# A graph network's softmax pass: one-hot rows made on ScalarE by Square and Relu, and 5 and 4 columns in turn looked up on TensorE in three groups

## The chip, the cores and the metric

One core of a Trainium2 chip. The metric is the device time of one execution in microseconds (us), shown as the median of three runs.

## What is computed

Four graph layers run one after the other over 6,250 nodes and 200,000 edges that are sorted by destination, each followed by a residual sum and a layer norm. The change is in the fourth, an attention layer with a softmax over the edges of each destination:

```python
z = x @ Wn
e = edge_attr @ We
s_src = (z @ att_src)[src]
s_dst = (z @ att_dst)[dst]
s_edge = e @ att_edge
score = jax.nn.leaky_relu(s_src + s_dst + s_edge, negative_slope=0.2)
max_per = jnp.maximum(jax.ops.segment_max(score, dst, num_segments=n), NEG)
score_exp = jnp.exp(score - max_per[dst])
denom = jax.ops.segment_sum(score_exp, dst, num_segments=n)
alpha = score_exp / (denom[dst] + 1e-08)
msg = (z[src] + e) * alpha[:, None]
out = jax.ops.segment_sum(msg, dst, num_segments=n)
return out + x
```

## The kernel before

`softmax_pass` walks over the edges in 98 blocks. The 128 partitions each own a stretch of the sorted edges, and a block is the next B = 16 edges ("columns") of every partition, 2,048 edges in all. The program's loop has IT = 49 turns of two blocks, h = 0 and h = 1. The text calls them the even block and the odd block. They have buffers of their own (names that end in 0 and 1), except the products `picked`, the messages `p_msg` and the PSUM banks `p_slots`.

Every edge needs the 65 numbers of its source node (`soft_table`: 64 features and a score). They come on two ways:

- **Gathered.** For B - K columns GpSimd issues one indirect DMA per column (L1744), with indices that ScalarE copies in `stage_index` (L1750). K is `KS[h]`, before 4 and 4, so 12 columns are gathered per block. GpSimd may start on block n + 2 only when block n's rows are used (`MADE`).
- **Looked up.** For the other K columns the table is held in SBUF in seven classes of 128 rows, each row holding 7 nodes, in two parts whose sum is exact (`parts`). `one_hots` makes for each class q a 0/1 matrix `one_lo[h][:, q, :]` by comparing the spread keys with that class's row numbers (`lanes`): seven `is_equal` passes on VectorE (L1810), each over K * 128 keys in 16-bit floats. TensorE multiplies it with the table: 7 classes x 2 parts = 14 matmuls a column (L1787), into one PSUM bank a column. VectorE then multiplies the bank with the 0/1 mask of the node within its row (`one_hi`, made by L1813) in `pick` (L1838), and adds up over the 7 in `gather` (L1841).

The four looked-up columns are in two groups of two: `multiply(h, 0)` goes to the banks `p_slots[0]`, `multiply(h, 1)` to `p_slots[1]`, and `pick(0)` and `pick(1)` empty them. Between the two groups TensorE turns the edge attributes of the block (L1801, two transposes).

The order of VectorE's work for block n is written out by hand. It goes: `pick(0)`; the seven one-hot passes for block n + 1 (L1810); the mask for n + 1 (L1813); `gather(0)`; `pen` and the carried top (L1860, L1861); the attributes' part of the score, which waits for TensorE's transposes (`turned`; L1864, L1866, L1868); `pick(1)`, `gather(1)`; seven small steps for the score, the running maximum and the exponents (L1878 to L1891). There it waits for ScalarE's Exp (L1769, L1770). Then come the messages (L1895 to L1900) and the segmented running sum, a scan over 81 x 16 numbers (L1905).

ScalarE does, for block n: wait for the gathers, copy the indices of block n + 2 (L1750), wait for the exponents (`SCORED`), two Exps, spread the factors for the scan (L1772), wait for the scan's end, copy the running rows out (L1776, L1777), and copy slots, keep and at_dst of block n + 2 (`stage`, L1753 to L1755). SyncE loads keys and attributes and stores the rows.

The semaphore `stepped` counts VectorE's steps, `per` of them a block, and everybody's waits for VectorE are counts of it: `FIRST_MADE` is `pick(0)`, `SECOND_MADE` is `pick(1)`, `SCORED` the exponents, `MADE` the messages of the features. `looked` counts TensorE's finished groups.

## Time and profile before

| | us |
|---|---|
| median of 3 runs | 13501.89 |
| the runs | 13510.13, 13501.60, 13501.89 |
| the profiled execution: span, first to last instruction | 13509.6 |
| TensorE (PE) busy | 9536.4 (71%) |
| VectorE (DVE) busy | 11066.4 (82%) |
| ScalarE (ACT) busy | 4374.5 (32%) |
| GpSimd (POOL) busy | 9266.9 (69%) |

The profiled execution's time as such is not listed apart; its span is 0.5 us under the slowest of the three runs and 7.7 us over the median, 0.06%. The shares are averages over all four layers. The softmax pass is the last large stage: its gathers are issued between 11856 us and 13382 us of the span, about 1530 us or 11% of it. In the rows PE is TensorE's matmuls, PEld its weight loads, and a line such as L1787 is a line of the kernel before.

### The profile page before, as it was taken

What the parts mean: (1) busy time and instruction counts of PE and PEld (TensorE: products, weight loads), DVE (VectorE), ACT (ScalarE), POOL (GpSimd) and SP (SyncE); (2) the same over time, 40 slices, a digit from 0 to 9 for tenths busy, and PEclk for the clock granted to TensorE, in tenths of its full rate; (3) what the DMA queues carried; (4) which work ended last, traced back from release to release, by engine and by line L of the source; (5) the groups of instructions that cost most, each with busy time, mean ns of one, the idle gap of its engine ahead of it and who ended that gap; (6) DMA issues with size and microseconds to landing.
All of it is one profiled execution on the core that took longest, in us unless ns stands there. A gap on an engine that the chain in (4) does not pass through costs nothing. (4 is left out here: it accounts for less than half of the span.)

```text
span 13509.6 us, 209667 instructions
## 1 busy us (share of the span) xinstructions
PE 9536.4 (71%) x57073; PEld 8046.3 (60%) x57073; DVE 11066.4 (82%) x24500; ACT 4374.5 (32%) x14847; POOL 9266.9 (69%) x9348
## 2 busy tenths in 40 slices
PE   5666667777757766777774546886886888678886
PEld 4555556666645555555552116886886777567775
DVE  8888878888768888888888997886886888589997
ACT  3444434444423333333333331111111111123332
POOL 6777757777667777777774005777776777677776
PEclk8888879999878888888886667998997999699997
DMA  3333324444323333333335761221221222133332
GB/s 89 89 89 85 88 71 125 124 119 124 113 65 100 99 101 101 101 100 97 99 101 195 272 246 41 48 47 39 47 48 38 50 49 49 30 78 87 85 87 68
DMA packets 637171, 1243.59 MB, mean 92 GB/s; under 512 B 206033, under 2 KB 390390, under 8 KB 586530
## 3 DMA queue, kind: packets, MB, share of 16 engines
q1 hardware_dynamic: 322624, 912.21, 19.9%
q0 software_dynamic: 300160, 269.02, 11.8%
q10 hardware_dynamic: 14337, 61.82, 1.2%
q8 instruction: 16, 0.26, 0.0%
q14 instruction: 34, 0.28, 0.0%
HBM read 475.84 MB, written 768.08 MB: 92 GB/s over the span
## 5 line engine op out<-in xcount | busy, mean ns | idle before, releaser
L1030 PE MATMUL p_slots<-part,one_lo 128*128 128x208 f32 (+1 forms) x18032 | 2666.9, 312 | 616.3 <-DVE one_lo L1048 615.9
L990 POOL DMA_INDIRECT rows<-gcn_table,index x2450 | 2442.6, 997 | 883.0 <-issue 727.7
L1030 PEld LDWEIGHTS p_slots<-part,one_lo 128*128 128x128 f32 x18032 | 2584.2, 205 | 699.2 <-DVE one_lo L1048 682.7
L1351 PE MATMUL a_p_slots<-att_part,a_one_lo 128*128 128x456 f32 x8232 | 2007.5, 408 | 585.2 <-DVE y L1414 502.8
L1351 PEld LDWEIGHTS a_p_slots<-att_part,a_one_lo 128*128 128x128 f32 x8232 | 1741.4, 214 | 953.6 <-DVE y L1414 680.7
L1282 POOL DMA_INDIRECT sent<-a_out_rows,a_place x1568 | 1585.5, 1011 | 494.0 <-issue 476.2
L622 PE MATMUL p_slots<-x_part,key_lo 128*128 128x448 f32 x6916 | 1649.2, 393 | 109.7 <-DVE scratch L751 73.3
L556 POOL DMA_INDIRECT msg<-x_rows,index x1372 | 1312.0, 956 | 507.4 <-issue 448.4
L556 POOL DMA_INDIRECT msg<-h_rows,index x1274 | 1234.4, 969 | 490.9 <-issue 383.8
L622 PEld LDWEIGHTS p_slots<-x_part,key_lo 128*128 128x128 f32 x6916 | 1378.1, 206 | 226.3 <-DVE scratch L751 90.3
L788 DVE SCALAR_TENSOR_TENSOR run<-run,keep,msg 128x129 f32<-128x129 f32 (+1 forms) x3136 | 1112.8, 355 | 388.7 <-ACT msg L591 284.2
L1744 POOL DMA_INDIRECT e_rows<-soft_table,e_index x1176 | 1167.4, 993 | 375.6 <-issue 330.8
L1787 PE MATMUL e_p_slots<-soft_part,e_one_lo 128*128 128x456 f32 x5488 | 1243.9, 387 | 125.2 <-DVE e_one_lo L1810 125.2
L1787 PEld LDWEIGHTS e_p_slots<-soft_part,e_one_lo 128*128 128x128 f32 x5488 | 1073.9, 198 | 260.3 <-DVE e_one_lo L1810 146.4
L1273 POOL DMA_INDIRECT a_rows<-att_table,a_index x980 | 998.9, 1019 | 305.7 <-issue 298.4
L1048 DVE TENSOR_SCALAR one_lo<-keys,lanes 128x1152 fp32r<-128x1152 f16 (+2 forms) x1188 | 826.4, 756 | 10.6 <-DMA keys<-key_rows 10.6
L996 ACT COPY index<-src_i 128x8 int32 (+4 forms) x300 | 59.2, 198 | 2286.4 <-DMA rows<-gcn_table,index 2176.6
L591 ACT ACTIVATE msg<-msg,weight 128x64 f32<-128x64 f32 x3136 | 769.1, 340 | 0.5 <-DVE msg L769 0.5
L584 ACT ACTIVATE earlier<-p_same 128x1280 bf16<-128x1280 f32 x392 | 485.2, 1238 | 787.8 <-PE p_same L637 787.8
L1078 DVE TENSOR_TENSOR picked<-p_slots,one_hi 128x832 f32<-128x832 f32 (+1 forms) x588 | 704.1, 1198 | 37.3 <-PE p_slots L1030 27.2
L1081 DVE TENSOR_REDUCE rows<-picked 128x64 f32<-128x832 f32 (+1 forms) x588 | 702.3, 1194 | 10.1
L1367 PE MATMUL a_p_label<-w_labels,a_label 128*128 128x512 f32 x392 | 340.8, 1021 | 467.4 <-DMA a_label_row<-in_label_rows 467.4
(478 smaller groups left out, 17203.7 us busy)
## 6 DMA issues: line engine op xcount, KB each, us to landing
running_dst<-a_run SPq DMA_DIRECT2D x98, 1600.0 KB
running_src<-s_run SPq DMA_DIRECT2D x98, 1600.0 KB
running<-run SPq DMA_DIRECT2D x98, 1032.0 KB
running<-run SPq DMA_DIRECT2D x98, 1024.0 KB
running<-y SPq DMA_DIRECT2D x98, 656.0 KB
s_rows<-sent ACTq DMA_DIRECT2D x98, 584.0 KB, 7.0
begun_x<-zeros SPq DMA_DIRECT2D x98, 512.0 KB
a_xdst<-begun_x SPq DMA_DIRECT2D x98, 512.0 KB
```

Source lines behind the costliest of these rows:

```text
L556: pool.indirect_dma_start(out=msg[h][:, K + k, 0:C], out_offset=None, in_=table, in_offset=offsets(index[h][:, k:k + 1])).then_inc(gathere ...
L591: nc.scalar.activation(msg[h][:, k, C:2 * C], msg[h][:, k, 0:C], ACT.Copy, scale=weight[h][:, k:k + 1]).then_inc(weighed, 1)
L622: ins = nc.tensor.matmul(p_slots[:, bank, 0:C * WIDE_CLASS], key_lo[h][:, c, e:e + P], flat(part[:, c, :, :]), start=c == 0 and part_no == ...
L788: step(nc.vector.scalar_tensor_tensor(run[h][:, k, :], before, keep[h][:, k:k + 1], msg[h][:, k, :], ALU.mult, ALU.add))
L990: pool.indirect_dma_start(out=rows[h][:, KS[h] + k, :], out_offset=None, in_=table, in_offset=offsets(index[h][:, k:k + 1])).then_inc(gath ...
L1030: ins = nc.tensor.matmul(to, one_lo[h][:, q, e:e + P], flat(part[:, q, :, :]), start=q == 0 and part_no == 0, stop=q == CLASSES - 1 and pa ...
L1048: step(nc.vector.tensor_scalar(one_lo[h][:, q, :], keys[h][:], sig["lanes"][:, q:q + 1], None, ALU.is_equal))
L1273: pool.indirect_dma_start(out=rows[h][:, K + k, :], out_offset=None, in_=table, in_offset=offsets(index[h][:, k:k + 1])).then_inc(gathered ...
L1282: pool.indirect_dma_start(out=sent, out_offset=offsets(place[h][:, k:k + 1]), in_=out_rows[h][:, k, :], in_offset=None).then_inc(scattered ...
L1351: ins = nc.tensor.matmul(to[:, k, 0:WIDE_COLUMNS], one_lo[h][:, q, e:e + P], part[:, q, :], start=q == 0 and part_no == 0, stop=q == WIDE_ ...
L1744: pool.indirect_dma_start(out=rows[h][:, KS[h] + k, :], out_offset=None, in_=table, in_offset=offsets(index[h][:, k:k + 1])).then_inc(gath ...
L1787: ins = nc.tensor.matmul(p_slots[g][:, k, 0:WIDE_COLUMNS], one_lo[h][:, q, e:e + P], part[:, q, :], start=q == 0 and part_no == 0, stop=q ...
```

## The change

In the softmax pass alone:

- `KS` becomes (5, 4): the even block looks up five columns and gathers 11, the odd block looks up four and gathers 12. TensorE has 70 and 56 matmuls a block where it had 56.
- The columns are in three groups: 2, 2, 1 in the even block and 2, 1, 1 in the odd one. The groups go in turn to two pairs of PSUM banks, `p_slots[(h + g) % 2]`, so that group 2 waits for `pick(0)` of its own block. TensorE's transposes stand behind group 1 and not behind group 0.
- VectorE has no one-hot passes in the loop any more. It has a third `pick` and a third `gather`.
- ScalarE makes the 0/1 rows in `light`: seven passes Square(2 * key + bias), with bias = -2 * lane, a pointer operand of one number a partition; and then one pass Relu(1 - x), in place over all seven classes (3,584 or 4,480 numbers a partition). The Relu waits for the last Square by a semaphore. In the turn of block n ScalarE first waits for TensorE's end of block n - 1 (`looked`), then does `light` for block n + 1, and only then what it did before.
- TensorE waits for `lit`, ScalarE's count of finished lights, and SyncE's loads of keys do too.
- One small pass at the start of the program makes `lane_bias`.

The diff:

```diff
-    KS = (4, 4)
+    KS = (5, 4)
     GATHERED = [B - K for K in KS]
-    FIRST = 2
-    GROUPS = [[slice(0, FIRST), slice(FIRST, K)] for K in KS]
-    MOST = [FIRST, max(KS) - FIRST]
-    FIRST_MADE, ONE_HOTS = 1, 1 + WIDE_CLASSES
-    SECOND_MADE = ONE_HOTS + 8
-    SCORED = SECOND_MADE + 8
+    GROUPS = [(slice(0, 2), slice(2, 4), slice(4, 5)), (slice(0, 2), slice(2, 3), slice(3, 4))]
+    G = 3
+    FIRST_MADE = 1
+    SECOND_MADE = FIRST_MADE + 8
+    THIRD_MADE = SECOND_MADE + 2
+    SCORED = THIRD_MADE + 8
...
-        picked = [sb(f"e_picked{g}", [P, MOST[g], Z, WIDE_CLASS]) for g in range(2)]
+        picked = pair("e_picked", [P, 2, Z, WIDE_CLASS])
...
-        p_slots = [ctx.enter_context(nc.psum_tensor(f"e_p_slots{g}", [P, MOST[g], 512], F32)) for g in range(2)]
+        p_slots = [ctx.enter_context(nc.psum_tensor(f"e_p_slots{g}", [P, 2, 512], F32)) for g in range(2)]
...
+        squared, lit = sig["squared"], sig["lit"]
...
-                sp.wait_ge(stepped, INIT + per * (n - 1) + ONE_HOTS)
+                sp.wait_ge(lit.sem, lit.base + n + 1)
                 load_keys(h, n + 2)
...
+            def light(h, n, loads):
+                act.wait_ge(spread_keys[h], 16 * loads)
+                for q in range(WIDE_CLASSES):
+                    ins = nc.scalar.activation(one_lo[h][:, q, :], keys[h][:], ACT.Square, bias=sig["lane_bias"][:, q:q + 1], scale=2.0)
+                ins.then_inc(squared.sem, 1)
+                act.wait_ge(squared.sem, squared.base + n + 1)
+                nc.scalar.activation(flat(one_lo[h][:]), flat(one_lo[h][:]), ACT.Relu, bias=sig["ones"][:, 0:1], scale=-1.0).then_inc(lit.sem, 1)
...
                 stage(h, h * B)
+            light(0, 0, 1)
             with act.Fori(0, IT) as i:
...
                     n = 2 * i + h
+                    act.wait_ge(looked, G * (n + 1))
+                    light(1 - h, n + 1, i + 1 + h)
...
                     stage_index(h, (n + 2) * B)
...
             def multiply(h, g):
-                for k in range(KS[h] - FIRST if g else FIRST):
-                    e = (g * FIRST + k) * P
+                cut, to = GROUPS[h][g], p_slots[(h + g) % 2]
+                for k in range(cut.stop - cut.start):
+                    e = (cut.start + k) * P
                     for q in range(WIDE_CLASSES):
                         for part_no, part in enumerate(parts):
-                            ins = nc.tensor.matmul(p_slots[g][:, k, 0:WIDE_COLUMNS], one_lo[h][:, q, e:e + P], part[:, q, :],
+                            ins = nc.tensor.matmul(to[:, k, 0:WIDE_COLUMNS], one_lo[h][:, q, e:e + P], part[:, q, :],
                                                    start=q == 0 and part_no == 0, stop=q == WIDE_CLASSES - 1 and part_no == len(parts) - 1)
...
+            pe.sem_inc(looked, G)
             with pe.Fori(0, IT) as i:
...
-                    pe.wait_ge(stepped, INIT + per * (n - 1) + ONE_HOTS)
+                    pe.wait_ge(lit.sem, lit.base + n + 1)
+                    pe.wait_ge(stepped, INIT + per * (n - 1) + SECOND_MADE)
                     multiply(h, 0)
+                    pe.wait_ge(stepped, INIT + per * (n - 1) + THIRD_MADE)
+                    multiply(h, 1)
...
                     pe.wait_ge(loaded[h], 16 * (B // PACK) * (i + 1))
...
-                    multiply(h, 1)
+                    pe.wait_ge(stepped, INIT + per * n + FIRST_MADE)
+                    multiply(h, 2)
...
-            def one_hots(h, step):
-                for q in range(WIDE_CLASSES):
-                    step(nc.vector.tensor_scalar(one_lo[h][:, q, :], keys[h][:], sig["lanes"][:, q:q + 1], None, ALU.is_equal))
             def one_slots(h, step):
...
             nc.vector.memset(run[1][:], 0.0).then_inc(stepped, per + FIRST_MADE)
-            dve.wait_ge(spread_keys[0], 16)
-            one_hots(0, lambda ins: ins.then_inc(stepped, 1))
             dve.wait_ge(staged[0], 1)
-            one_slots(0, lambda ins: ins.then_inc(stepped, per - ONE_HOTS))
+            one_slots(0, lambda ins: ins.then_inc(stepped, per - FIRST_MADE))
             with dve.Fori(0, IT) as i:
...
                     n, done = 2 * i + h, [0]
...
                     def pick(g):
-                        many = KS[h] - FIRST if g else FIRST
-                        slots = p_slots[g][:, 0:many, 0:Z * WIDE_CLASS].rearrange("p k (c s) -> p k c s", s=WIDE_CLASS)
+                        many = GROUPS[h][g].stop - GROUPS[h][g].start
+                        slots = p_slots[(h + g) % 2][:, 0:many, 0:Z * WIDE_CLASS].rearrange("p k (c s) -> p k c s", s=WIDE_CLASS)
                         mask = one_hi[h][:, GROUPS[h][g], :].unsqueeze(2).broadcast_to([P, many, Z, WIDE_CLASS])
-                        step(nc.vector.tensor_tensor(picked[g][:, 0:many, :, :], slots, mask, ALU.mult))
+                        dve.wait_ge(looked, G * (n + 1) + g + 1)
+                        step(nc.vector.tensor_tensor(picked[g % 2][:, 0:many, :, :], slots, mask, ALU.mult))
                     def gather(g):
-                        step(nc.vector.tensor_reduce(rows[h][:, GROUPS[h][g], 0:Z], picked[g][:, 0:KS[h] - FIRST if g else FIRST, :, :], AX.X, ALU.add))
+                        step(nc.vector.tensor_reduce(rows[h][:, GROUPS[h][g], 0:Z], picked[g % 2][:, 0:GROUPS[h][g].stop - GROUPS[h][g].start, :, :], AX.X, ALU.add))
...
-                    dve.wait_ge(looked, 2 * n + 1)
...
                     assert done[0] == FIRST_MADE
-                    dve.wait_ge(spread_keys[1 - h], 16 * (i + 1 + h))
-                    one_hots(1 - h, step)
-                    assert done[0] == ONE_HOTS
...
                     one_slots(1 - h, step)
...
-                    dve.wait_ge(looked, 2 * n + 2)
...
+                    pick(2)
+                    assert done[0] == THIRD_MADE
+                    after()
+                    gather(2)
...
+        squared.base += 2 * IT + 1
+        lit.base += 2 * IT + 1
...
         sig = {n: Signal(ctx.enter_context(nc.semaphore(n))) for n in
-               ("copied", "turned", "turned_sb", "product", "saved", "fetched", "pe_step", "act_step", "dve_step", "pool_step", "moved", "rounds")}
+               ("copied", "turned", "turned_sb", "product", "saved", "fetched", "pe_step", "act_step", "dve_step", "pool_step", "moved", "rounds", "squared", "lit")}
...
         sig["iota"], sig["lanes"] = sb("iota", [P, P]), sb("lanes", [P, WIDE_CLASSES])
+        sig["lane_bias"] = sb("lane_bias", [P, WIDE_CLASSES])
...
+                    step(V.tensor_scalar(sig["lane_bias"][:], sig["lanes"][:], -2.0, None, ALU.mult))
```

What the change does to the order on three engines, in the loop of the softmax pass, even block (buffer numbers are kept: e_keys1 are the odd block's keys).

ScalarE before, from the head of the loop's turn to the copy of the running rows (y):

```order
L1750 ACT_TABLE_LOAD
L1750 COPY e_index0<-src_i 128x12
L1768 ISA
L1769 ACTIVATE e_p_msg<-e_exps0 128x16
L1770 ACTIVATE e_factor0<-e_exps0 128x32
L1771 ISA
L1772 ACTIVATE e_carried<-e_factor0 128x81x15
L1774 ISA
L1775 REGISTER_ALU
L1776 ACTIVATE y<-e_run0 128x16x81
```

ScalarE in the changed kernel, from the same place:

```order
L1763 ACT_TABLE_LOAD
L1763 ACTIVATE e_one_lo1<-e_keys1,lane_bias 128x512 x7
L1765 REGISTER_ALU
L1766 ACTIVATE e_one_lo1<-e_one_lo1,ones 128x3584
L1780 REGISTER_ALU
L1752 ISA
L1752 COPY e_index0<-src_i 128x11
L1783 ISA
L1784 ACTIVATE e_p_msg<-e_exps0 128x16
L1785 ACTIVATE e_factor0<-e_exps0 128x32
L1786 ISA
L1787 ACTIVATE e_carried<-e_factor0 128x81x15
```

In front of the index copy and the Exp of the even block now stand the Squares and the Relu for the odd block. At the odd block's turn the same stands with 128x640 and 128x4480 numbers for the even block.

TensorE before, even block, around the transposes (L1801; part0 and part1 are the table's two parts):

```order
L1787 MATMUL e_p_slots0<-soft_part0,e_one_lo0 128x456
L1787 MATMUL e_p_slots0<-soft_part1,e_one_lo0 128x456
L1798 REGISTER_ALU
L1799 ISA
L1801 MATMUL e_p_attr<-ident,e_attr_t0 128x128 x2
L1787 MATMUL e_p_slots1<-soft_part0,e_one_lo0 128x456
L1787 MATMUL e_p_slots1<-soft_part1,e_one_lo0 128x456
```

TensorE in the changed kernel, even block, around the transposes (L1822):

```order
L1803 MATMUL e_p_slots1<-soft_part0,e_one_lo0 128x456
L1803 MATMUL e_p_slots1<-soft_part1,e_one_lo0 128x456
L1819 REGISTER_ALU
L1820 ISA
L1822 MATMUL e_p_attr<-ident,e_attr_t0 128x128 x2
L1825 ISA
L1803 MATMUL e_p_slots0<-soft_part0,e_one_lo0 128x456
```

The transposes stood behind group 0 (the 28 matmuls into e_p_slots0); they now stand behind groups 0 and 1, and the third group goes to e_p_slots0 again, behind one more wait (L1825).

VectorE before, even block, from the end of the attributes' part to the first score step:

```order
L1868 TENSOR_TENSOR e_edge_score0<-e_edge_score0,e_at_dst0 128x16
L1870 REGISTER_ALU
L1838 TENSOR_TENSOR e_picked1<-e_p_slots1,e_one_hi0 128x910
L1832 REGISTER_ALU
L1841 TENSOR_REDUCE e_rows0<-e_picked1 128x2x65
L1876 REGISTER_ALU
L1832 REGISTER_ALU
L1878 TENSOR_TENSOR e_score0<-e_rows0,e_edge_score0 128x16
```

VectorE in the changed kernel, the same place:

```order
L1881 TENSOR_TENSOR e_edge_score0<-e_edge_score0,e_at_dst0 128x16
L1855 REGISTER_ALU
L1856 TENSOR_TENSOR e_picked1<-e_p_slots1,e_one_hi0 128x910
L1848 REGISTER_ALU
L1859 TENSOR_REDUCE e_rows0<-e_picked1 128x2x65
L1855 REGISTER_ALU
L1856 TENSOR_TENSOR e_picked0<-e_p_slots0,e_one_hi0 128x455
L1848 REGISTER_ALU
L1859 TENSOR_REDUCE e_rows0<-e_picked0 128x65
L1892 REGISTER_ALU
L1848 REGISTER_ALU
L1894 TENSOR_TENSOR e_score0<-e_rows0,e_edge_score0 128x16
```

A half-size pick and a one-column gather have come in between `gather(1)` and the score; the seven one-hot passes that stood further ahead in the block are gone.

## Rows read from the trace of the kernel before

**Rows 1.** The pass as one stretch: us, busy (count) per engine, clock, DMA share, GB/s

```profile
11856.00:13390.00 1534.00, 1263.22 (x5684) 1091.09 (x5684) 1412.12 (x2850) 518.01 (x926) 1167.41 (x1176) 0.95 0.35 85
```

**Rows 2.** GpSimd's gathers, all blocks: ns min/median/max, first and last start

```profile
L1744 POOL DMA_INDIRECT e_rows<-soft_table,e_index x1176: 943/947/1311, 11856.3 to 13381.1; - x196
```

**Rows 3.** The waits in the pass: us in total, times, longest

```profile
POOL e_rows L1744 <- issue: 330.8, 1085, 0.3
```

**Rows 4.** Timeline of ScalarE: start us, us, line, work [idle before]

```profile
12001.35 0.20 ACT L1750 COPY e_index<-src_i 128x12 int32 x1
12001.47 0.19 ACT L1769 ACTIVATE e_p_msg<-e_exps 128x16 f32<-128x16 f32 x1
...
12001.84 1.22 ACT L1772 ACTIVATE e_carried<-e_factor 128x1215 f32<-128x1215 f32 x1
12006.88 2.53 ACT L1776 ACTIVATE y<-e_run 128x1296 f32<-128x1296 f32 x1 [3.82 <-DVE e_run L1905]
...
12009.60 0.23 ACT L1755 ACTIVATE e_at_dst<-at_dst 128x16 f32 x1
```

**Rows 5.** Timeline of VectorE, from a score to the next block's second gather

```profile
12000.04 0.18 DVE L1878 TENSOR_TENSOR e_score<-e_rows,e_edge_score 128x16 f32<-128x16 f32 x1 [0.43 <-DMA e_rows<-soft_table,e_index]
...
12001.84 1.23 DVE L1895 TENSOR_TENSOR e_p_msg<-e_rows,e_p_msg 128x1024 f32<-128x1024 f32 x1 [0.40 <-ACT e_factor L1770]
12002.98 0.43 DVE L1897 TENSOR_TENSOR e_p_msg<-e_p_attr,e_factor 128x256 f32<-128x256 f32 x1
...
12003.91 2.85 DVE L1905 TENSOR_TENSOR_SCAN e_run<-e_carried,e_p_msg 128x1296 f32<-128x1296 f32 x1
...
12007.82 2.93 DVE L1810 TENSOR_SCALAR e_one_lo<-e_keys,lanes 128x512 fp32r<-128x512 f16 x7
...
12011.92 0.41 DVE L1864 TENSOR_TENSOR e_weighted<-e_p_attr,w_edge_att 128x256 f32<-128x256 f32 x1
...
12012.92 1.11 DVE L1838 TENSOR_TENSOR e_picked<-e_p_slots,e_one_hi 128x910 f32<-128x910 f32 x1
12014.06 1.10 DVE L1841 TENSOR_REDUCE e_rows<-e_picked 128x130 f32<-128x910 f32 x1
```

**Rows 6.** VectorE's first message step, all blocks: ns min/median/max, first and last start

```profile
L1895 DVE TENSOR_TENSOR e_p_msg<-e_rows,e_p_msg x98: 1228/1229/1230, 11879.3 to 13386.6; 128x1024 f32<-128x1024 f32 x98
```

**Rows 7.** Timeline of ScalarE in the attention pass: scaled passes, a table load

```profile
5006.86 3.91 ACT L1312 ACTIVATE a_msg<-a_rows,a_att 128x64 f32<-128x64 f32 x16
5010.68 3.29 ACT L1312 ACTIVATE a_msg<-a_p_label,a_att 128x64 f32<-128x64 f32 x16
5013.99 1.28 ACT L1303 ACT_TABLE_LOAD   x1
```

**Rows 8.** Timeline of TensorE: 28 or 56 matmuls, transposes

```profile
11860.82 8.05 PE L1787 MATMUL e_p_slots<-soft_part,e_one_lo 128*128 128x456 f32 x28 [68.55 <-DVE e_one_lo L1810]
...
11868.85 11.85 PE L1787 MATMUL e_p_slots<-soft_part,e_one_lo 128*128 128x456 f32 x56
...
12003.46 0.44 PE L1801 MATMUL e_p_attr<-ident,e_attr_t 128*128 128x128 f32 x2 [1.88 <-DVE e_p_msg L1897]
12003.66 6.07 PE L1787 MATMUL e_p_slots<-soft_part,e_one_lo 128*128 128x456 f32 x28
...
5024.21 13.40 PE L1351 MATMUL a_p_slots<-att_part,a_one_lo 128*128 128x456 f32 x56 [4.59 <-DVE y L1414]
```

**Rows 9.** Granted clock (the 0.50 and 0.84) after a pause of TensorE's that ended at 5008.89

```profile
5008.00:5010.00 2.00, 1.11 (x2) 0.60 (x3) 2.00 (x10) 2.00 (x10) 1.70 (x2) 0.50 0.10 33
...
5014.00:5016.00 2.00, 2.00 (x10) 1.82 (x9) 2.00 (x4) 1.99 (x7) 1.39 (x3) 0.84 1.02 410
```

**Rows 10.** Start of the pass: VectorE's first ones, ScalarE's first Exp

```profile
11857.85 2.91 DVE L1810 TENSOR_SCALAR e_one_lo<-e_keys,lanes 128x512 fp32r<-128x512 f16 x7 [2.40 <-DMA e_keys<-wide_key_rows]
...
11878.96 0.19 ACT L1769 ACTIVATE e_p_msg<-e_exps 128x16 f32<-128x16 f32 x1 [3.87 <-DVE e_exps L1891]
```

## The prediction

> **What bounds the pass now.** I took the pass as one stretch first [rows 1]. In 1534 us VectorE is busy for 1412 us (92%), TensorE 1263 (82%), GpSimd 1167 (76%), ScalarE only 518 (34%). By shares VectorE would be the bound and ScalarE free. The waits say otherwise. GpSimd's idle time in front of its gathers is nearly all "issue": 330.8 us in 1085 pieces of at most 0.3 us [rows 3], waits for nobody. A gather takes 947 ns in the middle of its range [rows 2], plus that 0.3: 1.25 us, 12 of them 15.0 us, and the odd slow one on top. The 98 blocks start their messages from 11879.3 to 13386.6 us, 97 steps of 15.54 us [rows 6], or **31.08 us for a pair** of blocks. So GpSimd, issuing without a pause, sets the pace, and VectorE is close behind.
>
> I call E the start of a block's first Exp (12001.47 in [rows 4]). The tale of one block from E is what the change lengthens. The messages start 0.37 later, the scan at 12003.91 takes 2.85 [rows 5], ScalarE copies the rows out from 12006.88, and its last small copy starts at 12009.60 [rows 4]. One such copy blocks ScalarE for 0.11 (the one ahead of it starts that much earlier by the spacing of 0.12 between index copy and Exp in the same rows). So ScalarE is free at **E + 8.24**, and today idles for about 6 us.
>
> **What goes and what comes on VectorE and GpSimd.** Seven compares of 2.93 us [rows 5] leave VectorE in every block. A third pick and gather come: the pair looks up nine columns instead of eight, in six groups instead of four. Message steps of 1024 and 256 numbers take 1.23 and 0.43 [rows 5], so 455 numbers take 0.43 + 199 x 0.80 / 768 = 0.64. In the even block both new steps are whole additions (1.3 us), in the odd block a pick of two columns becomes two of one (2 x 0.64 against 1.11), some 0.35 more with the gathers. VectorE is relieved by about 2 us a block. GpSimd has 23 gathers a pair for 24: 31.08 x 23 / 24 = 29.8 us. Neither is worth anything unless ScalarE and TensorE keep that pace.
>
> **What comes on ScalarE.** In the attention pass 16 passes over 64 numbers with a pointer operand take 3.91 us, the last one about 0.33, so one starts 0.24 after the other [rows 7]. The slope: 1,215 numbers in 1.22 us against 16 in 0.19 [rows 4] give 0.86 ns a number; with the unrounded means of the two lines it is 0.85, which I take. A Square of 512 numbers then costs 0.24 + 448 x 0.00085 = 0.62, of 640 numbers 0.73. The Relu waits for the last Square, and stands alone: 0.33 + 3520 x 0.00085 = 3.32, or 4.08 for 4,480. With 0.13 for the last Square's end and the wait, light for the odd block is 4.34 + 0.13 + 3.32 = **7.79 us**, for the even block 5.10 + 0.13 + 4.08 = **9.31 us**. VectorE did four columns' classes in 2.93.
>
> The order rows show light in front of the index copy and the Exp. It is in nobody's shadow: ScalarE begins it when the last block's copies are out. The next E comes 0.03 after its end (0.12 for the index copy, less the overlap of 0.09). From an even E to the odd one, with the even block's light between: 8.24 + 9.31 + 0.03 = **17.58 us**. From odd to even, by ScalarE alone, with the table load of 1.28 [rows 7] and 0.12 of lost overlap: 8.24 + 1.40 + 7.79 + 0.03 = 17.46.
>
> **What TensorE adds.** It may not start the even block before that block's light is done, which is 0.03 before the odd E. At full clock 56 matmuls take 11.85, a spacing of 0.211; two transposes take 0.44 [rows 8]. The transposes now stand behind 56 matmuls, so the attributes are turned at odd E - 0.03 + 0.06 + 11.82 + 0.44 = 12.29, and VectorE waits for them. Then, by [rows 5]: 0.05 to begin, 1.00 to `pick(1)`, 1.14 to `gather(1)`, 1.10 for it, 0.67 for `pick(2)` with its wait, 0.66 for `gather(2)`, 1.43 from the first score step to the Exp (12000.04 to 12001.47). Even E is at odd E + **18.34**. Group 2 itself (14 more matmuls) is done at 15.2 and just hidden behind `pick(1)` and `gather(1)`, which end at 15.63. This beats ScalarE's 17.46, so the table load and the odd light are covered; if the ring through TensorE went, 17.46 would be next.
>
> **The clock.** TensorE starts the odd block about 17.5 after odd E, and is through its 56 matmuls some 12.2 us later, then idle until the next even light is done: about 8 us without a matmul in each pair. Before, pauses were some 2 us, the granted clock averaging 0.95 [rows 1]. After a pause of 4.59 us, 56 matmuls took 13.40 instead of 11.85, that is 1.55 more; after 68.55 us of nothing, 28 took 8.05 instead of 6.07, 1.98 more [rows 8]. In one place the clock stayed at its lower level (0.50) from the resumption at 5008.89 into 5014 to 5016, when it averaged 0.84 [rows 9]; half speed for 5.8 us loses 2.9. The cost is between nothing (the clock stays up) and 2.9 us. I take 1.98, since 8 us is longer than the 4.59. It falls on the even block's first matmuls, on the path: odd E to even E is 18.34 + 1.98 = **20.32 us**.
>
> **The sum.** The 97 steps: 49 x 17.58 + 48 x 20.32 = 1836.8 us against 1507.3, +329.5. The start: first ones began at 11857.85, first E was 11878.96 [rows 10]. Now light (9.31) ends at 11867.16, and the first E follows 20.35 later, at 11887.51: +8.5. The one pass that makes `lane_bias` is short and counted as 0.2. The tail after the last E is the same work. Together **+338 us**. The execution profiled had a span of 13509.6 us, so it would become about 13848; its own time is 0.06% over the median of the runs, and from the median 13501.9 I forecast **13840 us**.
>
> What is costed at nothing: SyncE's loads of keys wait for lit instead of VectorE's count; they are issued a block and more ahead of their Square. GpSimd's start on block n + 2 waits for `MADE` of n and for an index copy that now comes just before E: its 15 us have about 34. If either cover went, up to the overrun would be added.
>
> By the Trainium skill, ScalarE: Activation LUTs, section What ACT_TABLE_LOAD costs, a pass with a pointer operand takes 280 ns and 0.833 ns a number, and neighbours overlap by 93 ns. By these figures the even light is 9.2, the sum some 6 us lower; the rows stay in the sum. The same page's Rules for kernel authors would leave relu, mul and the like to VectorE, which speaks against this change, and the rows agree: 2.93 us there against 7.79 here for the same four columns.
>
> **Rivals.** (a) *The forecast*, ScalarE and TensorE in one ring with the clock falling once a pair: 52%. (b) *The same ring, but the clock stays up* at the even block's start or falls where nobody waits: 48 x 1.98 = 95 us less, 13745. For it: a pause of about 2 us in this pass cost nothing in the 28 matmuls at 12003.66. Against: the pause becomes four times as long. 22%. (c) *The clock stays low for longer*, as in [rows 9]: 0.92 more for 48 steps, 13884. 12%. (d) *Faster: ScalarE's passes over 16-bit keys are much cheaper than its rows.* The step from E to E would have to be under 14.9 for GpSimd to stay the bound; taking off 8.24, half a table load (0.70) and 0.03 leaves 5.9 us for an average light of 8.55, so it decides at 31% off. Then a pair is 29.8, 49 x 1.29 = 63 us less, 13439. For it: VectorE's compares of the same keys run at 0.82 ns a number with their overhead, faster than ScalarE's rows. Against: the Relu, 43% of light, reads 32-bit numbers. 5%. (e) *A light in between*, which lands within 0.2%: 4%. (f) *The change doesn't do what it says*: Square, Relu and Exp would need different tables, and loads of 1.40 come between them. The order shows one load a pair as before, so this would show only as an unforeseen slowdown, with other mishaps 5%: three more loads a pair, 4.2 x 49 = 206, 14046.
>
> **How the numbers follow.** 0.2% (27 us) is about what a measurement tells from no change. Faster 0.05, the same 0.04, slower 0.91. The range runs from (b) with 45 us off for lighter passes, 13700, to (c) with 20 on top, 13905; outside are (d), (e), (f).
>
> **What would show it.** Right: E to E alternates between about 17.6 and 20.3; GpSimd waits a few us in each block, for VectorE's messages; VectorE waits for the transposes in the even block and for Exp; ScalarE is busy some 90% of the pass; Squares near 0.7, Relus of 3.3 and 4.1; 28 matmuls after TensorE's long pause take about 8. Wrong: gathers still back to back, a light under 6, or a pair of 35.8 (then b).

## The result

| | before | changed |
|---|---|---|
| median, us | 13501.74 (4 runs) | 13861.31 (4 runs) |
| the runs, us | 13501.03 to 13510.13 | 13831.09, 13857.32, 13870.02, 13865.31 |
| the profiled execution: span, us | 13509.6 | 13829.3 |
| ratio, 95% interval | | 1.0263 (1.0248 to 1.0277) |

The changed kernel is 2.6% slower, 360 us by the medians; 13840 was forecast. The profiled execution is the fastest of the four.

The pass as one stretch in the changed kernel answers to [rows 1] (us, busy and count for PE, PEld, DVE, ACT and POOL, granted clock, DMA share, GB/s):

```profile
11856.00:13710.00 1854.00, 1443.77 (x6370) 1256.94 (x6370) 1207.47 (x2352) 1329.84 (x1718) 1062.45 (x1126) 0.86 0.28 71
```

ScalarE's busy time went from 518 to 1330 us, VectorE's fell from 1412 to 1207, and the pass is some 320 us longer with every engine less than 80% busy. The granted clock averages 0.86 for 0.95. No engine is full: the engines wait for one another in turn.

GpSimd's gathers in the changed kernel, by their tile (answers to [rows 2]; ns min/median/max, first and last start):

```profile
L1746 POOL DMA_INDIRECT e_rows<-soft_table,e_index x1127: 938/944/962, 11854.7 to 13685.2; - x188
```

The first Exp of all blocks in the changed kernel, by its tile, with the same columns (answers to [rows 6]):

```profile
L1784 ACT ACTIVATE e_p_msg<-e_exps x98: 175/183/189, 11886.2 to 13706.6; 128x16 f32<-128x16 f32 x98
```

From the first E to the last, 97 steps take 1820.4 us, **37.53 us for a pair** of blocks (31.08 before). The first E is at 11886.2.

The waits in the pass, us in total, times, longest (for [rows 3]):

```profile
PE e_p_slots L1803 <- ACT e_one_lo L1766: 448.0, 85, 74.8
ACT y L1791 <- DVE e_run L1921: 361.3, 97, 3.7
POOL e_rows L1746 <- issue: 313.6, 1029, 0.3
DVE e_p_msg L1911 <- ACT e_factor L1785: 178.3, 98, 3.2
DVE e_weighted L1877 <- PE e_p_attr L1822: 172.8, 49, 3.6
DVE e_picked L1856 <- PE e_p_slots L1803: 167.1, 49, 20.4
ACT e_p_msg L1784 <- DVE e_exps L1907: 153.1, 49, 11.8
```

TensorE waits 448 us for the Relu, 74.8 of them once, at the start of the pass. VectorE waits for ScalarE's factors, for TensorE's transposes and for its lookups, ScalarE for VectorE's exponents (each of these only in one of the two blocks of a pair, 49 times, the factors in both). GpSimd's largest wait is now for VectorE's messages (454.1 us in total in the same answer, at most 5.9 at a time). Before, no wait of its in the loop was longer than 0.3 us.

One pair on ScalarE (answers to [rows 4]; start us, us, line, work [idle before]):

```profile
12701.00 1.28 ACT L1763 ACT_TABLE_LOAD   x1
12702.30 4.41 ACT L1763 ACTIVATE e_one_lo<-e_keys,lane_bias 128x512 fp32r<-128x512 f16 x7
12706.73 3.29 ACT L1766 ACTIVATE e_one_lo<-e_one_lo,ones 128x3584 fp32r<-128x3584 f32 x1
...
12713.04 0.19 ACT L1784 ACTIVATE e_p_msg<-e_exps 128x16 f32<-128x16 f32 x1 [2.93 <-DVE e_exps L1907]
...
12721.15 5.13 ACT L1763 ACTIVATE e_one_lo<-e_keys,lane_bias 128x640 fp32r<-128x640 f16 x7
12726.31 4.03 ACT L1766 ACTIVATE e_one_lo<-e_one_lo,ones 128x4480 fp32r<-128x4480 f32 x1
12730.24 0.18 ACT L1752 COPY e_index<-src_i 128x12 int32 x1
12730.33 0.18 ACT L1784 ACTIVATE e_p_msg<-e_exps 128x16 f32<-128x16 f32 x1
...
12750.60 0.19 ACT L1784 ACTIVATE e_p_msg<-e_exps 128x16 f32<-128x16 f32 x1 [2.94 <-DVE e_exps L1907]
```

And on TensorE (for [rows 8]):

```profile
12710.15 8.97 PE L1803 MATMUL e_p_slots<-soft_part,e_one_lo 128*128 128x456 f32 x42 [0.16 <-ACT e_one_lo L1766]
12718.96 0.38 PE L1822 MATMUL e_p_attr<-ident,e_attr_t 128*128 128x128 f32 x2
12719.64 3.18 PE L1803 MATMUL e_p_slots<-soft_part,e_one_lo 128*128 128x456 f32 x14 [0.30 <-DVE e_picked L1856]
12730.48 13.94 PE L1803 MATMUL e_p_slots<-soft_part,e_one_lo 128*128 128x456 f32 x56 [7.66 <-ACT e_one_lo L1766]
```

E is at 12713.04 in the even block, 12730.33 in the odd one (0.09 behind the index copy, no idle time), and 12750.60 in the next even one, after 2.94 us of waiting. So the steps are **17.29** and **20.27 us**. TensorE stands still for 7.66 us in front of the even block, starts 0.14 us after the Relu ends (12726.31 + 4.03 = 12730.34), and its 56 matmuls take 13.94 instead of 11.85.

### The profile page after: what moved, and what is told of

The parts are those of the page before. It is cut to its first block and busy times, and to the rows that moved or that the text cites. A ratio compares the mean times of both kernels' runs of the same rounds, so it can differ in the third digit from the quotient of the medians.

```text
span 13829.3 us, 212219 instructions
## 1 busy us (share of the span) xinstructions
PE 9721.2 (70%) x57759; PEld 8214.9 (59%) x57759; DVE 10849.9 (78%) x24004; ACT 5185.4 (37%) x15639; POOL 9152.2 (66%) x9299
## 5 line engine op out<-in xcount | busy, mean ns | idle before, releaser
L1803 PE MATMUL e_p_slots<-soft_part,e_one_lo 128*128 128x456 f32 x6174 | 1433.1, 393 | 464.7 <-ACT e_one_lo L1766 448.0
L1803 PEld LDWEIGHTS e_p_slots<-soft_part,e_one_lo 128*128 128x128 f32 x6174 | 1231.0, 202 | 643.1 <-issue 485.3
L1746 POOL DMA_INDIRECT e_rows<-soft_table,e_index x1127 | 1063.4, 944 | 785.2 <-DVE e_p_msg L1916 454.1
```

What stands on the lines that cost most here:

```text
L1746: pool.indirect_dma_start(out=rows[h][:, KS[h] + k, :], out_offset=None, in_=table, in_offset=offsets(index[h][:, k:k + 1])).then_inc(gath ...
L1803: ins = nc.tensor.matmul(to[:, k, 0:WIDE_COLUMNS], one_lo[h][:, q, e:e + P], part[:, q, :], start=q == 0 and part_no == 0, stop=q == WIDE_ ...
```

## The experiments

The pair is (last E - first E) / 48.5 from each trace. The medians also hold what the other three layers do; their code is the same in all these kernels, yet the softmax pass's first gather came at 11856.3 us before, 11854.7 in the changed kernel and at up to 11912.5 (e11) in the others. Most of that arises, where I compared it, in the second turn of the first layer, whose last gathers were issued at 3640.4 and 3687.3 us after starts at 1964.4 and 1964.3 (before, e6). Where medians and pairs differ, that is why, and the pair is the measure of the pass.

| kernel | pair, us | median, us | before, measured beside it | ratio (interval) |
|---|---|---|---|---|
| before | 31.08 | 13501.74 | | |
| changed | 37.53 | 13861.31 | 13501.74 | 1.0263 (1.0248 to 1.0277) |
| e1 light behind Exp | 33.74 | 13678.39 | 13506.83 | 1.0126 (1.0109 to 1.0143) |
| e2 four columns | 34.14 | 13686.31 | 13506.83 | 1.0133 (1.0116 to 1.0150) |
| e3 pause filled | 35.83 | 13770.25 | 13506.83 | 1.0196 (1.0179 to 1.0213) |
| e4 ones on VectorE | 32.43 | 13608.83 | 13506.83 | 1.0071 (1.0054 to 1.0088) |
| e5 e1, keys early | **29.19** | **13441.62** | 13514.61 | 0.9948 (0.9934 to 0.9961) |
| e6 e5, four columns | 29.81 | 13475.64 | 13514.61 | 0.9971 (0.9960 to 0.9982) |
| e7 no Relu (one run) | 34.05 | 13698.7 | 13514.61 | |
| e8 transposes back (one run) | 37.52 | 13836.24 | 13514.61 | |
| e9 e5, transposes back | 30.97 | 13529.31 | 13492.71 | 1.0029 (1.0017 to 1.0041) |
| e10 e9, attributes early | 29.14 | 13455.18 | 13506.92 | 0.9961 (0.9947 to 0.9974) |
| e11 e5, attributes early | 29.16 | 13443.19 | 13506.92 | 0.9954 (0.9941 to 0.9968) |

The theory under test is the forecast's ring: light stands in front of Exp, TensorE's even block waits for light, and in that pause the clock falls. The rivals are that the new work itself is too much (the fifth column on TensorE, the third group, ScalarE's passes beside the others), whatever its order.

**e1: light behind Exp, one block further ahead.**

```diff
             light(0, 0, 1)
+            light(1, 1, 1)
...
-                    act.wait_ge(looked, G * (n + 1))
-                    light(1 - h, n + 1, i + 1 + h)
                     act.wait_ge(gathered[h], 16 * GATHERED[h] * (i + 1))
...
                     nc.scalar.activation(carried[:, :, 1:B], repeat(factor[h][:, B + 1:2 * B], S), ACT.Copy).then_inc(activated, 1)
+                    stage(h, (n + 2) * B)
+                    act.wait_ge(looked, G * (n + 2))
+                    light(h, n + 2, i + 2)
                     act.wait_ge(stepped, INIT + per * (n + 1))
...
-                    stage(h, (n + 2) * B)
```

> Same work as the changed kernel; only ScalarE's order differs: its small copies (stage) and light now stand between the factors' spreading and the copy of the running rows, and light makes the ones of the block after next, into the buffer that TensorE has just finished. Ring theory (light stands in front of Exp, and TensorE's even block waits for it): both delays vanish, ScalarE needs 28.4 us a pair, TensorE about 27, VectorE about 28, and GpSimd's 23 gathers set the pace at 29.8 us a pair, so 13440 us or a little more, under the kernel before. Rival (the amount of work is the trouble: ScalarE's passes slow VectorE or TensorE down, or five columns are too many for TensorE): the pair stays above 33 us and the time above 13600.

Missed: the pair fell by 3.8 us, half of what was expected, to 33.74, and both numbers of the rival held ("above 33", "above 13600"; 13678 us measured). By this run alone the rival was not refuted. ScalarE's waits, us in total, times, longest:

```profile
ACT e_one_lo L1763 <- DMA e_keys<-wide_key_rows: 315.5, 98, 4.4
```

Every light stood 3.2 us in the mean for its keys, a wait that I had costed at nothing. SyncE loads them in the turn after the store of the block before, and that store waits for ScalarE's copy of the rows, which e1 had pushed back behind light. The edit had made its own new ring through SyncE's queue; e5 takes it out.

**e5: the keys one turn earlier.** On top of e1 (with one load more ahead of the loop):

```diff
-                sp.wait_ge(lit.sem, lit.base + n + 1)
-                load_keys(h, n + 2)
+                sp.wait_ge(lit.sem, lit.base + n + 2)
+                load_keys(1 - h, n + 3)
```

> e1_ahead with SyncE's load of the keys moved one block forward: while block n runs it loads the keys of n + 3 as soon as the light of n + 1 is done, ahead of the store of block n. In e1 every light waited 3 to 4 us for its keys, 315.5 us in all, because the load stood behind the store of the block before. Ring theory: that wait was the whole of what kept e1 at 33.7 us a pair; ScalarE now needs 28.4 us, TensorE 27, VectorE 27 to 28, and GpSimd's 23 gathers set the pace: 29.8 to 30.5 us a pair, and with 8 us more at the start of the pass 13430 to 13480, under the kernel before. Rival (light cannot be hidden at all, each engine's work being longer beside the others): 32 us a pair or more, 13560 and up.

The pair is 29.19 us, under the 29.8 to 30.5 expected (e6 shows why) and 1.89 less than before the change. The time is inside the band, 0.52% under the kernel before (ratio 0.9948, 0.9934 to 0.9961). The kernel does all the work of the changed one, in another order. That refutes the rivals of too much work: what cost 360 us was where light stood. e5's pass from 12000 to 13300 us, with the columns of [rows 1]:

```profile
12000.00:13300.00 1300.00, 1206.68 (x5793) 1066.78 (x5792) 1103.90 (x2134) 1192.38 (x1555) 968.72 (x1024) 1.00 0.36 92
```

ScalarE is busy for 92% of it, and the clock is at its upper level throughout (1.00). ScalarE's light for an even block, the copy of the rows behind it, and the next two Exps, of the odd and the even block:

```profile
12715.90 5.13 ACT L1765 ACTIVATE e_one_lo<-e_keys,lane_bias 128x640 fp32r<-128x640 f16 x7
12721.07 4.04 ACT L1768 ACTIVATE e_one_lo<-e_one_lo,ones 128x4480 fp32r<-128x4480 f32 x1
12725.01 2.46 ACT L1795 ACTIVATE y<-e_run 128x1296 f32<-128x1296 f32 x1
...
12727.56 0.18 ACT L1784 ACTIVATE e_p_msg<-e_exps 128x16 f32<-128x16 f32 x1
...
12743.32 0.19 ACT L1784 ACTIVATE e_p_msg<-e_exps 128x16 f32<-128x16 f32 x1 [2.23 <-DVE e_exps L1910]
```

**e2: four columns in both blocks.**

```diff
-    KS = (5, 4)
+    KS = (4, 4)
...
-    GROUPS = [(slice(0, 2), slice(2, 4), slice(4, 5)), (slice(0, 2), slice(2, 3), slice(3, 4))]
+    GROUPS = [(slice(0, 2), slice(2, 3), slice(3, 4))] * 2
```

> The changed kernel with four columns in both blocks, groups of 2, 1, 1. Ring theory: light is 7.7 us in both blocks and TensorE's block is 14 matmuls shorter, so TensorE is no longer the later one: from E to E 16.0 us, and 17.4 with the table load, 33.4 us a pair (31.08 before), some 115 us over the kernel before, 13615. If the fifth column's matmuls and gathers were the trouble and ScalarE's work were covered, the pair would be 31.1 and the time 13500.

The pair is 34.14, 0.7 over what was expected (the median is 71 us over, of which the pairs are 36), 3.4 under the changed kernel and 3.1 over the one before. So about half of the loss goes with the fifth column, which lengthens the even light and TensorE's chain, and half is there without it. e2 alone doesn't tell the amount of work from its place; e5, with all five columns, does. The 0.7 lies in one step, 16.89 for 16.0: there Exp waits 1.00 us for VectorE's exponents, and TensorE's matmuls ahead of them took 1.88 more than at full clock, which that expectation had left out. TensorE in one block with the pause and in the next without:

```profile
12709.60 10.84 PE L1803 MATMUL e_p_slots<-soft_part,e_one_lo 128*128 128x456 f32 x42 [6.20 <-ACT e_one_lo L1766]
...
12725.42 8.96 PE L1803 MATMUL e_p_slots<-soft_part,e_one_lo 128*128 128x456 f32 x42 [1.85 <-DVE e_score L1896]
```

The 42 matmuls take 10.84 after a pause of 6.20 us and 8.96 after one of 1.85, so TensorE's chain outlasts ScalarE's in the step without a table load. The other step, 17.23 for 17.4, is ScalarE's, with no wait in front of Exp.

**e3: TensorE kept at work in the pause.**

```diff
-                    pe.wait_ge(lit.sem, lit.base + n + 1)
                     pe.wait_ge(stepped, INIT + per * (n - 1) + SECOND_MADE)
+                    if h == 0:
+                        for _ in range(27):
+                            nc.tensor.matmul(p_slots[0][:, 0, 0:WIDE_COLUMNS], parts[0][:, 0, 0:P], parts[0][:, 0, :], start=True, stop=True)
+                    pe.wait_ge(lit.sem, lit.base + n + 1)
                     multiply(h, 0)
```

> The changed kernel with 27 extra matmuls (5.7 us at full clock) of the table with itself, into the bank that group 0 overwrites afterwards, in TensorE's pause ahead of each even block, behind the wait for VectorE's second pick and ahead of the wait for light. Their results are not used. If the clock's fall in the pause costs 2 us a pair as forecast, the 56 matmuls take 11.9 instead of 13.9 us, a pair 35.5 us and the time falls by about 95 us, to 13765. If the clock costs nothing on the path, the time stays within 15 us of the changed kernel; if the extra matmuls come in the way, it rises.

TensorE's timeline in e3:

```profile
12705.21 5.90 PE L1815 MATMUL e_p_slots<-soft_part 128*128 128x456 f32 x27 [0.75 <-DVE e_picked L1859]
12711.40 11.87 PE L1803 MATMUL e_p_slots<-soft_part,e_one_lo 128*128 128x456 f32 x56 [0.28 <-ACT e_one_lo L1766]
...
12728.64 10.53 PE L1803 MATMUL e_p_slots<-soft_part,e_one_lo 128*128 128x456 f32 x42 [2.23 <-ACT e_one_lo L1766]
```

Right: 56 matmuls in 11.87 instead of 13.94 (L1815 is the filling), and 91 us less by the medians, though 1,323 matmuls were added. The pairs alone give 1.70 x 48.5 = 82 us. The pair shown takes 35.41 us by its steps, the mean is 35.83; in some odd blocks the clock now falls instead (42 matmuls in 10.53 for 8.96).

**e4: ones on VectorE again**, all else as changed.

```diff
-                sp.wait_ge(lit.sem, lit.base + n + 1)
+                sp.wait_ge(stepped, INIT + per * (n - 1) + ONE_HOTS)
...
-                    act.wait_ge(looked, G * (n + 1))
-                    light(1 - h, n + 1, i + 1 + h)
...
-                    pe.wait_ge(lit.sem, lit.base + n + 1)
                     pe.wait_ge(stepped, INIT + per * (n - 1) + SECOND_MADE)
...
                     assert done[0] == FIRST_MADE
+                    dve.wait_ge(spread_keys[1 - h], 16 * (i + 1 + h))
+                    one_hots(1 - h, step)
```

> The changed kernel with the ones made on VectorE again, at the place where the kernel before makes them; five and four columns, three groups and the two pairs of banks stay. Ring theory: the loss was ScalarE's light, so it is nearly gone: VectorE, 14.4 us busy a block before, gets 1.7 us a pair for the third picks and gathers and 0.4 for the fifth column's ones, and sets the pace at 31.5 to 32.5 us a pair, 13520 to 13570. Rival (the third group and its waits, or the fifth column on TensorE, made most of the loss): over 13700.

The pair of 32.43 is inside what was expected; the median is 39 us over the expected band's end, and the profiled execution shows why: its pass begins at 11891.4, 35 us later than before. VectorE is busy 94% of the time and sets the pace. So of the change's 6.45 us a pair, 1.35 remain without ScalarE's light.

**e7: no Relu.** The Relu is left out, so the lookup multiplies with squares.

```diff
-                ins.then_inc(squared.sem, 1)
-                act.wait_ge(squared.sem, squared.base + n + 1)
-                nc.scalar.activation(flat(one_lo[h][:]), flat(one_lo[h][:]), ACT.Relu, bias=sig["ones"][:, 0:1], scale=-1.0).then_inc(lit.sem, 1)
+                ins.then_inc(lit.sem, 1)
```

> The changed kernel without the Relu (left out: its pass over the classes, so the rows are squares, not ones). Light is 4.5 and 5.2 us. Ring theory: from even to odd E ScalarE's chain falls from 17.3 to 13.2 us; from odd to even E TensorE's chain stays at 18.3, with the clock's loss up to 20.3; the pair 31.6 to 33.5 us, 180 to 270 us less in the pass, and GpSimd waits less. If light stood in nobody's way, the pair would stay at 37.5.

ScalarE's timeline in e7:

```profile
12706.21 0.19 ACT L1782 ACTIVATE e_p_msg<-e_exps 128x16 f32<-128x16 f32 x1 [5.70 <-DVE e_exps L1905]
...
12720.64 0.19 ACT L1782 ACTIVATE e_p_msg<-e_exps 128x16 f32<-128x16 f32 x1 [1.13 <-DVE e_exps L1905]
...
12740.33 0.19 ACT L1782 ACTIVATE e_p_msg<-e_exps 128x16 f32<-128x16 f32 x1 [5.69 <-DVE e_exps L1905]
```

TensorE's in e7:

```profile
12719.56 14.60 PE L1801 MATMUL e_p_slots<-soft_part,e_one_lo 128*128 128x456 f32 x56 [3.58 <-ACT e_one_lo L1763]
```

The pair of 34.05 is 0.55 over what was expected, the pass 169 us shorter for 180 to 270. Even to odd E fell from 17.29 to 14.43, by 2.9 and not 4.1: E now waits 1.13 us for VectorE's exponents. They come 14.4 us after the even E in both kernels, so VectorE's chain had been 2.9 us shorter than ScalarE's and is now the longer one. Odd to even is 19.69 for 20.27, as expected of TensorE's chain. Its pause is only 3.58 us and yet 56 matmuls take 14.60, 2.75 over full clock: the loss is no function of the pause alone.

**e8: transposes behind group 0**, as in the kernel before, all else as changed.

```diff
                     multiply(h, 0)

-                    pe.wait_ge(stepped, INIT + per * (n - 1) + THIRD_MADE)
-                    multiply(h, 1)
-
                     pe.wait_ge(stepped, INIT + per * (n - 1) + MADE + 1)
                     pe.wait_ge(loaded[h], 16 * (B // PACK) * (i + 1))
...
                     ins.then_inc(turned, 1)
+
+                    pe.wait_ge(stepped, INIT + per * (n - 1) + THIRD_MADE)
+                    multiply(h, 1)
```

> The changed kernel with TensorE's transposes behind group 0 again. By the forecast's working VectorE's wait for the transposes was the last one in the even block, with the fifth column's matmuls just hidden: odd to even E falls from 20.3 to about 19.9 us (pick 2 then waits for its matmuls instead), even to odd stays at 17.3, the pair 37.1. If the waits for the transposes don't matter it stays at 37.5; a clock that falls at another moment can move it by as much.

The pair is 37.52 and the steps are the same as changed, 17.29 and 20.24. TensorE's first group after the pause took 8.36 (28 matmuls), 2.3 over full clock, where the changed kernel lost 2.09:

```profile
12697.94 8.36 PE L1803 MATMUL e_p_slots<-soft_part,e_one_lo 128*128 128x456 f32 x28 [7.68 <-ACT e_one_lo L1766]
```

VectorE no longer waits for the transposes. Its third pick waits 0.66 us for TensorE's third group instead and starts 17.48 us after the odd E, where the changed kernel's starts at 17.52. Without the clock's loss that is 15.2 as worked out, against 15.4 in the changed kernel. So of the 0.4 us that the working found, half was never there and half went to the clock.

**e9, e10, e11: loads and transposes on top of e5.** e9 is e5 with e8's edit.

> e5 with TensorE's transposes behind group 0. In e5 VectorE waits 1.9 us for them in each even block and ScalarE 2.2 us for the exponents that come of it, with the clock at its upper level all through. Here, where no fall of the clock can eat the gain as in e8, the even block's wait goes: the pair falls from 29.19 us to what GpSimd's 23 gathers and their 0.3 us allow, 28.7 to 28.9, 15 to 25 us in all, about 13420. If GpSimd was already the bound in e5, nothing changes (29.2).

Wrong, and worse: 30.97. TensorE's weight load for the transposes found a new wait, us in total, times, longest:

```profile
PEld e_p_attr L1822 <- DMA e_attr_t<-in_attrs: 90.0, 43, 2.7
```

The attributes land too late for that place: SyncE loads them behind the store of the rows. In e10 both loads come ahead of the store, with e9's transposes (the edit is shown against e9); e11 has the same loads and the transposes where e5 has them:

```diff
-            def store(h, i):
+            def store(h, i, more):
                 n = 2 * i + h

-                sp.wait_ge(lit.sem, lit.base + n + 2)
+                sp.wait_ge(lit.sem, lit.base + n + 3)
                 load_keys(1 - h, n + 3)
+                if more:
+                    load(h, n + 2)

                 sp.wait_ge(copied, n + 3)
...
-                    load(h, 2 * i + 2 + h)
```

> e9 with SyncE's loads of keys and attributes both ahead of the store, behind the light of n + 2. In e9 TensorE's transposes, moved forward, found the attributes not landed (DMA, 2.1 us a pair) because their load stood behind the store of the rows, and the pair went from 29.19 up to 30.97 us. If that late load was the whole of it, the wait goes and the pair is 28.8 to 29.0 us, the time 13415 to 13430. If it stays near 31, something else in the order of the transposes costs.

> e10 with the transposes behind group 1, where the change puts them (so e5 with the loads forward alone). In e5 no wait for the attributes showed, so this should be e5 again: 29.1 to 29.3 us a pair, 13435 to 13450.

29.14 and 29.16: the late load was the whole of e9's loss, and the transposes' place earns nothing. e11 came out as expected; e10 missed its 28.8 to 29.0 (its median is 25 us over the band; it is 12 over e11's, but their runs overlap, and the pairs are alike). By the trace, what holds e10 at 29.14 is the same ring as in the forecast, only closed over two blocks; no run cut it. ScalarE's timeline in e10:

```profile
12716.01 0.19 ACT L1784 ACTIVATE e_p_msg<-e_exps 128x16 f32<-128x16 f32 x1 [2.20 <-DVE e_exps L1911]
...
12717.82 5.13 ACT L1765 ACTIVATE e_one_lo<-e_keys,lane_bias 128x640 fp32r<-128x640 f16 x7
12722.98 4.04 ACT L1768 ACTIVATE e_one_lo<-e_one_lo,ones 128x4480 fp32r<-128x4480 f32 x1
...
12745.19 0.19 ACT L1784 ACTIVATE e_p_msg<-e_exps 128x16 f32<-128x16 f32 x1 [2.20 <-DVE e_exps L1911]
```

TensorE's in e10:

```profile
12727.16 6.08 PE L1806 MATMUL e_p_slots<-soft_part,e_one_lo 128*128 128x456 f32 x28 [1.36 <-ACT e_one_lo L1768]
```

From even E (12716.01) the light for the next even block ends 11.0 us later, TensorE starts on it at once (1.36 us idle) and its chain to the next even E takes 18.2: 29.2 us together, just above GpSimd's 23 gathers with their 0.3 us of issue (28.7).

**e6: e5 with four columns** (e2's edit on top of e5's).

> e5 with four looked-up columns in both blocks. If GpSimd sets e5's pace, its 24 gathers a pair set this one's: 31.1 us a pair, 13505 to 13520, and e5 is 1.3 us a pair (63 us) faster. If ScalarE or TensorE set e5's pace, this one is as fast as e5 or faster.

Neither. GpSimd does set e6's pace (VectorE waits 151.0 us for its gathers in the trace), but 24 gathers take 29.81 us, not 31.08, and the fifth column earns 0.62 us a pair. Moving the ones off VectorE had made the gathers themselves faster.

## Why the forecast held

- **GpSimd bound before**: yes by the trace, where none of its waits in the loop is over 0.3 us. e6, with the same 24 gathers, runs at their pace too, which has become faster.
- **Light**: 9.31 and 7.79 us forecast; 12721.15 to 12730.34 is 9.19, 12702.30 to 12710.02 is 7.72. By the Trainium skill, ScalarE: Activation LUTs, section What ACT_TABLE_LOAD costs, 280 ns and 0.833 ns a number give 9.2 and 7.7 as an estimate, which the trace bears out more closely than my rows. A single table load took 1.28 here as before.
- **Even to odd E, ScalarE's chain**: 17.58 forecast, 17.29 measured. ScalarE was free at E + 8.11 (8.24), and light was 0.12 shorter.
- **Odd to even, TensorE's chain**: 18.34 + 1.98 forecast, 20.27 measured. e7 shows that it stands when ScalarE's chain is cut. The forecast had the transposes as the last wait in it, with the fifth column's matmuls 0.4 us ahead; e8 shows the two within 0.2 us of each other, so moving the transposes alone gains nothing.
- **The clock**: 1.98 us on the even block's first matmuls forecast, 2.09 measured; e3 gives it back on that block. That its medians give 91 us for the forecast's 95 is in part chance, as the pairs give 82: in some odd blocks the clock falls instead. The forecast took 1.98 because the pause would be longer than one that cost 1.55, but the cost doesn't rise with the pause (last section), so that the size fits is luck in part. Rival (b), the ring without the clock's fall, is close to what e3 shows: 35.83 us a pair, where the forecast names 35.8 (17.58 + 18.34 make 35.9).
- **The start**: first E at 11887.5 forecast, 11886.2 measured.
- **The sum**: +338 forecast. The profiled execution is 321 us over 13510.13: 7.2 from the start of the pass, 313.2 from the 97 steps (329.5 forecast, each step 0.05 to 0.3 shorter than worked out). So the mechanism came out 17 us too long, and the median of 13861 lies 21 over the 13840 only with what the other runs add. The median rose by 360; the three other runs are 26 to 39 us above the profiled one. Whether that lies in the other layers or in the clock of this pass isn't shown, as they have no trace.
- **Mis-sized**: the pace of GpSimd, "31.08 x 23 / 24 = 29.8 us". It scaled the slow gathers too, and these went with the ones: 29.81 is what 24 gathers took in e6. It touched rival (d) and what was expected of e1, e5 and e6, not the sum. Also "SyncE's loads of keys ... are issued a block and more ahead": true of the changed kernel (2.9 us of waiting in the pass, all of it at the start), but not of any reordering, as e1 showed.

## What to carry to other kernels

An engine at a third of its time can still be the worst place for more work: ask in front of which wait the new work stands, not how much idle time the engine has. With the same 8.5 us of passes a block the change cost 360 us when they stood in front of the step that VectorE waits for, and gained 0.5% when they stood behind it, with their product made one block further ahead. When work is moved, follow each queue that it is moved past: two of the reorderings here (e1 and e9) lost half or all of their gain to a load that stood behind a store on SyncE's queue.

## What the hardware showed that was not expected

**Gathers slow down beside VectorE's one-hot compares.** The groups of GpSimd's work from 11870 to 13290 us, the line of the gathers alone (count, busy us, mean ns), in the kernel before:

```profile
L1744 POOL DMA_INDIRECT e_rows<-soft_table,e_index x1095 | 1087.0, 993 | 333.9 <-issue 308.3 <-DVE e_p_msg L1897 12.2 <-DVE e_p_msg L1898 7.0
```

The same in the changed kernel:

```profile
L1746 POOL DMA_INDIRECT e_rows<-soft_table,e_index x872 | 822.8, 944 | 598.6 <-DVE e_p_msg L1916 355.7 <-issue 242.6 <-ACT e_index L1752 0.3
```

In e4:

```profile
L1747 POOL DMA_INDIRECT e_rows<-soft_table,e_index x996 | 980.4, 984 | 436.2 <-issue 277.8 <-DVE e_p_msg L1913 141.1 <-DVE e_run L1826 17.3
```

In e6:

```profile
L1748 POOL DMA_INDIRECT e_rows<-soft_table,e_index x1110 | 1047.7, 944 | 355.2 <-issue 312.4 <-DVE e_one_hi L1834 17.3 <-DVE e_p_msg L1917 13.7
```

Where VectorE makes the ones (before, e4) a gather takes 993 and 984 ns in the mean; where ScalarE does (changed, e6) 944. The slow ones fall on the seven compares, as here before the change, where VectorE's line L1810 runs from 12007.82 to 12010.75:

```profile
12007.19 0.95 POOL L1744 DMA_INDIRECT e_rows<-soft_table,e_index  x1 [0.30 <-issue]
12008.44 1.24 POOL L1744 DMA_INDIRECT e_rows<-soft_table,e_index  x1 [0.30 <-issue]
12009.99 1.18 POOL L1744 DMA_INDIRECT e_rows<-soft_table,e_index  x1 [0.30 <-issue]
12011.48 0.94 POOL L1744 DMA_INDIRECT e_rows<-soft_table,e_index  x1 [0.30 <-issue]
```

By 24 gathers that is 1.2 us a pair, the 1.27 by which e6 is faster than before. What in the compares does it was not tried. One compare of 512 numbers takes 2.93 / 7 = 0.42 us, and the two gathers beside them took 0.2 to 0.3 us more than the others. The Trainium skill has a cause to offer, in SBUF — State Buffer, section Who interferes with whom: a VectorE operation in a mode that uses both of its ports, which operations such as these compares can enter, holds a pair of ports that GpSimd needs too, to write its DMAs' descriptors, and the other waits. That each gather loses less than one compare's time agrees with it, but no row tells the mode that the compares ran in, and no run here separates this from another cause, such as the memory that both read.

**The clock's loss isn't proportional to the pause.** After pauses of 1.85, 2.23, 3.58, 6.20 and 7.66 us the matmuls behind them took 0, 1.57, 2.75, 1.88 and 2.09 us more than at full clock (e2, e3, e7, e2, changed). The granted clock, the third number from the end of a row, shows what the pause alone doesn't. In the changed kernel it falls during the pause (TensorE stands still from 12722.8 to 12730.48) and is back at its upper level at about 12735:

```profile
12724.00:12725.00 1.00, 0.00 (x0) 0.00 (x0) 0.97 (x3) 1.00 (x3) 0.83 (x1) 0.90 0.78 151
...
12735.00:12736.00 1.00, 1.00 (x7) 0.91 (x6) 0.62 (x1) 0.34 (x1) 0.77 (x1) 0.98 0.18 34
```

In e7 (still from 12716.0 to 12719.56):

```profile
12718.00:12719.00 1.00, 0.00 (x0) 0.00 (x0) 0.97 (x2) 1.00 (x2) 0.69 (x2) 0.87 0.73 140
...
12725.00:12726.00 1.00, 1.00 (x5) 0.86 (x4) 0.94 (x1) 0.03 (x1) 0.69 (x2) 0.72 0.10 13
```

Between the rows shown it is 0.50, its lower level, in every microsecond. So it was low for 5.7 us of the changed kernel's pause, but only for the last 0.8 us of e7's, and the matmuls ran at the lower level for 4.6 and for 6.0 us. Half of that, less some 0.2, is what they lost. So they pay for the part of the low stretch that lies behind the pause. In e2, whose clock is low from 12706.9 to 12713.7, that part is 4.1 us. Why the low stretch is 10.2 us long in the changed kernel and 6.8 in e2 and e7 isn't shown. In e5, with pauses of 1.4 us and less, the granted clock stayed at its upper level (1.00), where the kernel before averaged 0.95 with pauses of about 2 us.
